# Reading context and x straight from the inputs instead of from copies in DRAM, in a fused mLSTM and FP4 FFN kernel

## The chip, the core and the metric

The kernel runs on one core of one Trainium2 chip. A core has a matrix engine (PE, with its weight loads PEld), a vector engine (DVE), a scalar engine (ACT), a general engine (POOL) and SyncE (SP), which computes nothing and issues transfers. Each engine works off its own instructions in order and waits on semaphores that others raise. ACT can issue transfers too: its sequencer does that, in the place where they stand in ACT's order. Transfers run on 16 DMA engines that all queues share. The metric is the device time of one execution in microseconds (us), lower is better.

## The reference, cut to what matters

For x and a context of shape (8, 1024, 512) the layer computes an mLSTM cross attention with causal decay gates, then a feed forward part whose matrices and activations are rounded to FP4 in blocks of 16:

```
x = x + xattn(layernorm(x), ctx, ctx, igate, fgate, norm_w)
x = x + ffn(layernorm(x), w_gate, w_up, w_down)

xattn: ig, fg = gates of concat(q, k, v);  log_f_cum = cumsum(log_sigmoid(fg))
       D = exp(log_D - max(log_D));  C = (q k^T / 8) * D
       h = C / max(|sum C|, exp(-max)) @ v;  per-head normalisation, times norm_w
ffn:   fp4_linear(h, w_down),  h = silu(fp4_linear(x, w_gate)) * fp4_linear(x, w_up)
fp4_linear(x, w): both quantised in blocks of 16 (scale = max|.|/6, 8 levels), then x @ w^T
```

The attention has 8 heads of width 64; the inner width of the feed forward part is 1408.

## The kernel before, in words

**Tiles.** The 8 x 1024 tokens make 64 tiles of 128 rows. Tile `t` holds 64 tokens (`t.chunk = t // 4`) of batch `2p` in the upper 64 partitions and of batch `2p + 1` in the lower 64 (`t.p = t % 4`). Four tiles after one another cover the same 64 positions of all 8 batches. Such a group of four is also what the gates are computed for at once.

**Turns.** After a prologue (`sp_start`, `act_start`, `dve_start`, ...), which quantises the weights and brings up the first tiles, every engine runs turns `u` from 10 on, each with a fixed order of steps of several tiles: tile `u + 1` is loaded, `u` gets its first layer norm, `u - 1` is transposed, `u - 5` and `u - 6` are in the attention, `u - 7` to `u - 10` are in the feed forward part. So a turn finishes one tile. The order in a turn is written out by hand for each engine (`sp_turn`, `act_turn`, `dve_turn`, ...). Turns with `u % 4 == 0` also do the gate work of a group of four (called gate turns below), turns with `u % 4 == 1` store its rows of maxima and exponentials (`sp_rows_out`).

**What is loaded.** For each tile from the 10th on: `xb` (x for the first layer norm, `sp_x_in`), `cf` (context in blocks of 32 x 32 so that DVE can transpose it into `cT`, `sp_c_in`, four transfers of 32 rows), `cn` (context rows for `vc`, in which the two batch halves are swapped for every other head, `sp_cn_in`), `x1` (x a second time, for the residual, `sp_x1_in`) and broadcasts of the stored gate rows (`mb_in`, `wb_in`). `xb` goes through DRAM once more (`xh_out`, `xz_in`) to come back in the order that DVE's transpose wants.

**The copies.** In turns with `u % 4 == 1`, up to `u = 57`, ACT issues five transfers from DRAM to DRAM ahead of anything else in its turn (`act_stage_x` at L1081, `act_stage_c` at L1074): x and context of the next group of four tiles are written tile by tile into `x_tiles` and `c_tiles`, context with a third half so that `cn` can be read with its halves swapped. The outermost dimension of each copy is the four tiles; it moves 4 x 64 rows of 2 KB. Two groups of such copies are issued in the prologue. `cf` and `cn` are read from `c_tiles` from tile 8 on, `xb` and `x1` from `x_tiles` from tile 12 on.

**Names that come up.** On ACT: L833 the exponentials of `D` (8 instructions), L958 the layer norm of x (`act_xh`), L1007 `hz` (two pieces at the turn's start), L848 to L869 mean and variance of the second layer norm, whose result POOL's L1232 (`rs`) takes. On POOL: L1268 and L1272 (`nb`, which `act_xh` waits for), L1241 `vc` from `cn`, L1257 `xw` from `wb`. On DVE: L1438 and L1443 round the hidden values, L1483 `xs`, L1420 the output, L1746 the transpose of `cf`. On PE: L592 gate and up products, L689 to L729 the attention's products, L748 to L750 the down product.

Of the kernel before, what the change touches and what calls it, by code (L numbers as in the profile page):

```python
# [9 lines left out]
F32 = mybir.dt.float32  # L10
# [65 lines left out]
def mlstm_fp4_ffn(nc, x, ctx_in, ig_w, ig_b, fg_w, fg_b, norm_w, w_gate, w_up, w_down, out):  # L76
# [20 lines left out]
    warp_dram = nc.dram_tensor("warp_dram", [NT // 4, GR * S2], F32, kind="Internal").ap()  # L97

    x_tiles = nc.dram_tensor("x_tiles", [NT, P, E], F32, kind="Internal").ap()
    c_tiles = nc.dram_tensor("c_tiles", [NT, 3 * S2, E], F32, kind="Internal").ap()  # L100

    def tokens(dram, t, b):
        return dram[2 * t.p + b, t.chunk * S2:(t.chunk + 1) * S2, :]

    with ExitStack() as stack:
# [28 lines left out]
        cT = sb("cT", [P, 8, EC, P])  # L134
# [125 lines left out]
        def state_sum(t, b):  # L260
# [16 lines left out]
            "x_in", "c_in", "cn_in", "x_tiles", "c_tiles", "mb_in", "wb_in", "max_out", "warp_out",  # L277
# [22 lines left out]

        def x_staged(t):
            return t.first >= 12

        def c_staged(t):
            return t.first >= 8

        def x_count(t):
            return 64 + 32 * min(t.first - 3, 8) + 16 * max(t.first - 11, 0)

        def x1_count(t):  # L310
            return 32 * min(t.chunk + 1, 3) + 16 * max(t.chunk - 2, 0)

        def cn_count(t):
            return 64 * min(t.first + 1, 8) + 32 * max(t.first - 7, 0)
# [23 lines left out]
        def sp_stored(e, t):  # L338
            e.wait_ge(S_["out"], t.done())
            for b in range(2):  # L340
                e.dma_start(tokens(out, t, b), ob[t.parity][b * S2:(b + 1) * S2, :]).then_inc(s_stored[t.parity], 16)

        def sp_x1_in(e, t):
            if t.at_start(2):
                e.wait_ge(S_["w_qs"], 3 * NG)
            if t.at_start(3):
                e.wait_ge(S_["w_xn"], 3 * NG)
            if t.has(4):
                e.wait_ge(S_["out"], t.done(4))
            if x_staged(t):  # L350
                e.wait_ge(S_["x_tiles"], 32 * (t.chunk - 2))
                e.dma_start(x1[t.slot % 4][:, :], x_tiles[t.first]).then_inc(s_x1_in[t.slot % 4], 16)
                return
            for b in range(2):
                e.dma_start(x1[t.slot % 4][b * S2:(b + 1) * S2, :], tokens(x, t, b)).then_inc(s_x1_in[t.slot % 4], 16)
# [10 lines left out]
        def sp_x_in(e, t):  # L366

            if t.first < 4:
                for b in range(2):
                    e.dma_start(xin(t)[b * S2:(b + 1) * S2, :], tokens(x, t, b)).then_inc(S_["x_in"], 16)  # L370
                return
# [4 lines left out]
            if x_staged(t):  # L376
                e.wait_ge(S_["x_tiles"], 32 * (t.chunk - 2))
                e.dma_start(xb[:, :], x_tiles[t.first]).then_inc(S_["x_in"], 16)
                return
            for b in range(2):  # L380
                e.dma_start(xb[b * S2:(b + 1) * S2, :], tokens(x, t, b)).then_inc(S_["x_in"], 16)
# [15 lines left out]
        def sp_c_in(e, t):  # L397
            if not blocked(t):
                if t.has(1):
                    e.wait_ge(S_["c_T"], t.done(1))  # L400
                for b in range(2):
                    e.dma_start(cf[b * S2:(b + 1) * S2, :], tokens(ctx_in, t, b)).then_inc(S_["c_in"], 16)
                return
            e.wait_ge(S_["cT"], t.done(1))
            e.wait_ge(S_["c_tiles"], 48 * (t.chunk - 1))
            rows = c_tiles[t.first][0:P, :].rearrange("(q s) (k g f) -> g s k q f", s=SQ, g=P // SQ, f=SQ)
            for g in range(P // SQ):
                e.dma_start(cf[g * SQ:(g + 1) * SQ, :].rearrange("s (k q f) -> s k q f", k=EC, f=SQ), rows[g]).then_inc(S_["cz_in"], 16)

        def sp_mb_in(e, t):  # L410
# [4 lines left out]
            e.wait_ge(S_["max_out"], t.dma(4))  # L415
            for k in range(2):
                at = (4 * k + t.p) * NH * S2
                e.dma_start(mb[k * S2:(k + 1) * S2, :, :].rearrange("p h s -> p (h s)"),
                            max_dram[t.chunk:t.chunk + 1, at:at + NH * S2].broadcast_to([S2, NH * S2])).then_inc(S_["mb_in"], 16)
# [12 lines left out]
        def sp_rows_out(e, t):  # L432
            if t.slot % 4 == 3:
# [3 lines left out]
                e.dma_start(warp_dram[t.chunk, :].rearrange("(r s) -> r s", s=S2), mw[:, 1, :]).then_inc(S_["warp_out"], 16)  # L437

        def sp_wb_in(e, t):
# [5 lines left out]
            e.wait_ge(S_["warp_out"], t.dma(4))  # L445
            for par in range(2):
                for b in range(2):
                    at = (((par ^ b) * 4 + t.p) * 2 + par) * HC * S2
                    e.dma_start(wb[par * DH:(par + 1) * DH, b, :, :].rearrange("p c s -> p (c s)"),
                                warp_dram[t.chunk:t.chunk + 1, at:at + HC * S2].broadcast_to([DH, HC * S2])).then_inc(S_["wb_in"], 16)  # L450

        def sp_cn_in(e, t):
# [3 lines left out]
            if c_staged(t):  # L456
                e.wait_ge(S_["c_tiles"], 48 * (t.chunk - 1))
                for par in range(2):
                    e.dma_start(cn[:, :].rearrange("s (c r d) -> s r c d", r=2, d=DH)[:, par],
                                c_tiles[t.first][par * S2:par * S2 + P, :].rearrange("s (c r d) -> s r c d", r=2, d=DH)[:, par]).then_inc(S_["cn_in"], 16)  # L460
                return
            for par in range(2):
                for b in range(2):
                    k = par ^ b
                    e.dma_start(cn[k * S2:(k + 1) * S2, :].rearrange("s (c r d) -> s r c d", r=2, d=DH)[:, par],
                                tokens(ctx_in, t, b).rearrange("s (c r d) -> s r c d", r=2, d=DH)[:, par]).then_inc(S_["cn_in"], 16)
# [25 lines left out]
        def sp_turn(e, u):  # L492
# [11 lines left out]
            if t6.live(NT):  # L504
                sp_cn_in(e, t6)
# [13 lines left out]
            if t6.live(NT):  # L519
                sp_x1_in(e, t6)  # L520
# [74 lines left out]
        def pe_qk(e, t):  # L595
# [1323 lines left out]
```

## Time and profile before

| | us |
|---|---|
| median of 2 runs | 2229.48 (2228.14 to 2230.83) |
| the profiled execution | 2230.32 |
| its span, first to last instruction | 2228.6 |

In that span DVE is busy for 1811.8 us (81%), PE for 1752.1 (79%), POOL for 1220.3 (55%) and ACT for 1154.4 (52%). The span is what the trace shows; the profiled execution's own time is 1.7 us longer. Busy is the time in which an engine executes an instruction, also where that instruction is held up inside by another engine. "Idle before" and the name behind it tell which event ended an engine's idle time.

### The profile page before, as it was taken

What the parts mean: (1) busy time and instruction counts of PE and PEld (TensorE: products, weight loads), DVE (VectorE), ACT (ScalarE), POOL (GpSimd) and SP (SyncE); (2) the same over time, 40 slices, a digit from 0 to 9 for tenths busy, and PEclk for the clock granted to TensorE, in tenths of its full rate; (3) what the DMA queues carried; (4) which work ended last, traced back from release to release, by engine and by line L of the source; (5) the groups of instructions that cost most, each with busy time, mean ns of one, the idle gap of its engine ahead of it and who ended that gap; (6) DMA issues with size and microseconds to landing.
All of it is one profiled execution on the core that took longest, in us unless ns stands there. A gap on an engine that the chain in (4) does not pass through costs nothing. (4 is left out here: it accounts for less than half of the span.)

```text
span 2228.6 us, 46871 instructions
## 1 busy us (share of the span) xinstructions
PE 1752.1 (79%) x16113; PEld 912.3 (41%) x16113; DVE 1811.8 (81%) x3327; ACT 1154.4 (52%) x2602; POOL 1220.3 (55%) x1260
## 2 busy tenths in 40 slices
PE   4444887869879696887869878686987869989998
PEld 3322443434434343443434444343443434444443
DVE  7953986959789695986969689595987959999996
ACT  7643553545555363563645456363554645655542
POOL 7843654636456463654546465463654646666663
PEclk8566988989989898998989989898999989999999
DMA  6395545546455564646545465554645545554333
GB/s 185 90 116 78 127 105 132 122 112 122 120 124 119 128 123 110 136 113 131 120 117 124 112 132 117 126 126 115 132 109 125 122 123 121 117 119 86 88 77 63
DMA packets 647726, 259.86 MB, mean 117 GB/s; under 512 B 581248, under 2 KB 603264, under 8 KB 646944
## 3 DMA queue, kind: packets, MB, share of 16 engines
q1 hardware_dynamic: 646672, 221.21, 48.6%
q10 hardware_dynamic: 816, 35.65, 3.8%
q8 instruction: 128, 2.10, 0.4%
q14 instruction: 110, 0.90, 0.1%
HBM read 159.22 MB, written 67.37 MB: 102 GB/s over the span
## 5 line engine op out<-in xcount | busy, mean ns | idle before, releaser
L592 PE MATMUL bank<-wgTh,xqT 128*128 128x512 f16 (+1 forms) x1536 | 579.7, 377 | 165.0 <-DMA xqT<-xqs 107.0
L592 PE MATMUL bank<-wuTh,xqT 128*128 128x512 f16 (+1 forms) x1536 | 578.0, 376 | 0.0
L1224 POOL TENSOR_TENSOR stage<-stage,hs 128x512 f32<-128x512 f32 (+1 forms) x192 | 213.4, 1111 | 304.4 <-DVE stage L1443 303.1
L592 PEld LDWEIGHTS bank<-wgTh,xqT 128*128 128x128 f16 x1536 | 155.0, 101 | 351.3 <-DMA xqT<-xqs 97.4
L592 PE MATMUL bank<-wgTl,xqT 128*128 128x512 f16 (+1 forms) x768 | 288.9, 376 | 0.0
L592 PE MATMUL bank<-wuTl,xqT 128*128 128x512 f16 (+1 forms) x768 | 288.2, 375 | 0.0
L748 PE MATMUL bank<-wdTh,work 128*128 128x512 f16 x704 | 269.8, 383 | 23.1 <-DMA work<-stage 22.6
L749 PE MATMUL bank<-wdTl,work 128*128 128x512 f16 x704 | 268.6, 382 | 0.0
L750 PE MATMUL bank<-wdTh,work 128*128 128x512 f16 x704 | 268.4, 381 | 0.0
L1279 POOL TENSOR_TENSOR stage<-stage,hinv 128x512 f32<-128x512 f32 (+1 forms) x192 | 210.5, 1109 | 30.7 <-DVE hinv L1542 24.1
L592 PEld LDWEIGHTS bank<-wuTh,xqT 128*128 128x128 f16 x1536 | 155.5, 101 | 154.4 <-issue 19.0
L1483 DVE TENSOR_SCALAR xs<-xam,rs 128x32 f32<-128x32 f32 x64 | 206.9, 3233 | 2.2
L934 ACT ACTIVATE junk<-xb 128x512 bf16<-128x512 f32 x60 | 37.8, 629 | 321.3 <-DMA xb<-x_tiles 313.4
L1241 POOL TENSOR_TENSOR vc<-cn,cols 128x512 f32<-128x512 f32 x64 | 66.8, 1043 | 231.4 <-DMA cn<-c_tiles 202.1
L1462 DVE SCALAR_TENSOR_TENSOR stage<-bank,wfix,stage 128x512 f32<-128x512 f32 (+1 forms) x192 | 134.1, 698 | 68.5 <-ACT stage L886 68.4
L689 PE MATMUL bank<-St,xw 64*64 64x65 f32 x2048 | 54.4, 248 | 170.5 <-DVE mb_D L1454 167.2
L886 ACT ACTIVATE stage<-bank,wfix 128x512 f32<-128x512 f32 (+1 forms) x192 | 124.5, 648 | 115.4 <-PE bank L592 113.4
L1746 DVE STREAM_TRANSPOSE cT<-cf 128x512 f32<-128x512 f32 x55 | 38.4, 698 | 171.4 <-DMA cf<-c_tiles 171.4
L1443 DVE SCALAR_TENSOR_TENSOR stage<-work,stage 128x512 f32<-128x512 bf16 (+1 forms) x192 | 164.0, 881 | 2.3
L1497 DVE TENSOR_TENSOR stage<-stage 128x512 f16<-128x512 f32 (+1 forms) x192 | 134.3, 699 | 37.6 <-ACT stage L876 37.6
L1204 POOL TENSOR_TENSOR sch<-ve,mhalf 128x8 f32<-128x8 f32 x64 | 106.2, 1659 | 98.9 <-DVE ve L1660 98.9
L1218 POOL TENSOR_TENSOR St<-St,wb 128x520 f32<-128x520 f32 x64 | 73.9, 1154 | 143.6 <-PE bank L695 143.6
(215 smaller groups left out, 3978.2 us busy)
## 6 DMA issues: line engine op xcount, KB each, us to landing
wb<-warp_dram SPq DMA_DIRECT2D x256, 64.0 KB, 2.9
mb_D<-max_dram SPq DMA_DIRECT2D x128, 128.0 KB, 3.2
out_dram<-ob SPq DMA_DIRECT2D x128, 128.0 KB, 2.4
cn<-c_tiles SPq DMA_DIRECT2D x112, 128.0 KB, 2.9
xh_dram<-xb SPq DMA_DIRECT2D x55, 256.0 KB, 2.4
xzb<-xh_dram SPq DMA_DIRECT2D x220, 64.0 KB, 2.5
cf<-c_tiles SPq DMA_DIRECT2D x220, 64.0 KB, 2.5
xb<-x_tiles SPq DMA_DIRECT2D x52, 256.0 KB, 2.7
```

What stands on the lines that cost most here:

```text
L592: i = e.matmul(o[:, 0:width], x, w[:, c, n0:n0 + width], start=first and k < 2, stop=last and k >= 4)
L748: e.matmul(acc[:, :], hi, wdT[0][:, c0 + c, :], start=(c0 + c == 0), stop=False)
L749: e.matmul(acc[:, :], hi, wdT[1][:, c0 + c, :], start=False, stop=False)
L750: i = e.matmul(acc[:, :], lo, wdT[0][:, c0 + c, :], start=False, stop=(c0 + c == IC - 1))
L886: e.activation(sl[:, n0:n0 + w], pair(t, n)[0][:, 0:w], ACT.Silu, scale=wfix[:, 0:1]).then_inc(s_silu[n], 1)
L1204: e.tensor_tensor(sch[:, :], ve[:, :], mhalf[:, :], ALU.pow).then_inc(S_["sch"], 1)
L1224: e.tensor_tensor(blocks(hx[:, n0:n0 + w]), blocks(hx[:, n0:n0 + w]), per_block(hs2[:, n0 // BLOCK:(n0 + w) // BLOCK]), ALU.mult).then_inc ...
L1279: e.tensor_tensor(blocks(hx[:, n0:n0 + w]), blocks(hb[:, n0:n0 + w]), per_block(hinv[:, n0 // BLOCK:(n0 + w) // BLOCK]), ALU.mult).then_in ...
L1443: e.scalar_tensor_tensor(hx[:, n0:n0 + w], hz[:, n0:n0 + w], MAGIC, hx[:, n0:n0 + w], ALU.max, ALU.subtract).then_inc(s_h_q[n], 1)
L1462: e.scalar_tensor_tensor(hb[:, n0:n0 + w], pair(t, n)[1][:, 0:w], wfix[:, 1:2], sl[:, n0:n0 + w], ALU.mult, ALU.mult).then_inc(s_h[n], 1)
L1483: e.tensor_scalar(xs[:, :], xam[:, :], rs2[:, :], 6.0 * XS * 1e-12, ALU.mult, ALU.max).then_inc(S_["xs"], 1)
L1497: e.tensor_tensor(hqs[n][:, 1, :], hx[:, n0:n0 + w], hqs[n][:, 0, :], ALU.subtract).then_inc(s_h_lo[n], 1)
```

## The change

The copies in DRAM, their tensors and semaphores are gone. Every load of x and context reads the input itself, with one transfer for each batch half: `xb` and `x1` in 2 transfers of 64 rows where there was 1 of 128, `cf` in 8 of 32 rows with half the columns each where there were 4, `cn` in 4 of 64 rows where there were 2 of 128. `cT` gets a dimension for the batch half, and the products that read it follow. `wb` comes in 2 transfers instead of 4, for which the stored row is written half again behind itself (one more transfer per group). In the turns, `cn` and `x1` are issued by ACT instead of SP: `cn` right behind `act_xh`, `x1` in the middle of the turn. In the prologue SP still issues them.

```diff
-        def tokens(dram, t, b):
-            return dram[2 * t.p + b, t.chunk * S2:(t.chunk + 1) * S2, :]
+    def tokens(dram, t):
+        return dram[2 * t.p:2 * t.p + 2, t.chunk * S2:(t.chunk + 1) * S2, :]
...
-            if x_staged(t):
-                e.wait_ge(S_["x_tiles"], 32 * (t.chunk - 2))
-                e.dma_start(xb[:, :], x_tiles[t.first]).then_inc(S_["x_in"], 16)
-                return
             for b in range(2):
-                e.dma_start(xb[b * S2:(b + 1) * S2, :], tokens(x, t, b)).then_inc(S_["x_in"], 16)
+                e.dma_start(xb[HALF[b], :], tokens(x, t)[b]).then_inc(S_["x_in"], 16)
...
-            e.wait_ge(S_["c_tiles"], 48 * (t.chunk - 1))
-            rows = c_tiles[t.first][0:P, :].rearrange("(q s) (k g f) -> g s k q f", s=SQ, g=P // SQ, f=SQ)
+            rows = tokens(ctx_in, t).rearrange("b (q s) (k g f) -> g b s k q f", s=SQ, g=P // SQ, f=SQ)
             for g in range(P // SQ):
-                e.dma_start(cf[g * SQ:(g + 1) * SQ, :].rearrange("s (k q f) -> s k q f", k=EC, f=SQ), rows[g]).then_inc(S_["cz_in"], 16)
+                for b in range(2):
+                    e.dma_start(cf[g * SQ:(g + 1) * SQ, b * E // 2:(b + 1) * E // 2].rearrange("s (k q f) -> s k q f", k=EC, f=SQ), rows[g, b]).then_inc(S_["cz_in"], 16)
...
+            for par in range(2):
+                row = warp_dram[t.chunk, :].rearrange("(k n r i) -> k n r i", k=3, n=4, r=2)[par:par + 2, t.p, par, :]
+                e.dma_start(wb[par * DH:(par + 1) * DH, :, :, :].rearrange("p b c s -> p (b c s)"),
+                            row.unsqueeze(0).broadcast_to([DH, 2, HC * S2])).then_inc(S_["wb_in"], 16)
+
+        def cn_load(e, t):
+            if t.has(1):
+                e.wait_ge(S_["vc"], t.done(1))
+                e.wait_ge(S_["st_mm"], t.done(1))
+            to = cn[:, :].rearrange("p (c r d) -> p r c d", r=2, d=DH)
+            rows = tokens(ctx_in, t).rearrange("b s (c r d) -> r b s c d", r=2, d=DH)
             for par in range(2):
                 for b in range(2):
...
+                    e.dma_start(to[HALF[par ^ b], par], rows[par, b]).then_inc(S_["cn_in"], 16)
...
         def act_turn(e, u):
             tn = Tile(u + 1)
-            g = (u + 3) // 4
-            if u % 4 == 1 and 4 * g < NT:
-                act_stage_x(e, g)
-                act_stage_c(e, g)
...
             if t0.live(NT):
                 act_xh(e, t0)
+            if t6.live(NT):
+                cn_load(e, t6)
             if t9.live(NT):
                 act_hz(e, t9, 1)
...
             if t9.live(NT):
                 act_hz(e, t9, 2)
                 act_h_hi(e, t9, 1)
+            if t6.live(NT):
+                x1_load(e, t6)
```

The next piece is SP's order in one turn of the middle of the run (`xqT` opens the turn; `cf` and `cn` are context, `x` is the second load of x), before:

```order
L430 DMA_TRANSPOSE xqT<-xqs 128x8x128
L459 DMA cn<-c_tiles 128x4x64 x2
L449 DMA wb<-warp_dram 64x256 x4
L408 DMA cf<-c_tiles 32x16x32 x4
L387 DMA xh_dram<-xb 128x512
L378 DMA xb<-x_tiles 128x512
L395 DMA xzb<-xh_dram 32x16x32 x4
L341 DMA out_dram<-ob 64x512 x2
L352 DMA x<-x_tiles 128x512
L364 DMA_TRANSPOSE work<-stage 128x8x128 x2
```

And the same stretch of the changed program:

```order
L402 DMA_TRANSPOSE xqT<-xqs 128x8x128
L422 DMA wb<-warp_dram 64x2x256 x2
L381 DMA cf<-in_ctx_dram 32x8x32 x8
L360 DMA xh_dram<-xb 128x512
L354 DMA xb<-in_x_dram 64x512 x2
L368 DMA xzb<-xh_dram 32x16x32 x4
L322 DMA out_dram<-ob 64x512 x2
L341 DMA_TRANSPOSE work<-stage 128x8x128 x2
```

`cn` and `x` have left SP's queue, `wb` has two issues less, `cf` four more and `xb` one more: 16 issues in this stretch, which were 17.

The second place is the start of ACT's turn, from the exponentials of `D` to the variance of the second layer norm, with the semaphores that each instruction waits for, before:

```order
L833 ACTIVATE mb_D<-mb_D,cols 128x64 x7
L958 ACTIVATE xb<-xb,nb,rs 128x512 [waits s_ln1,s_ln1_nb]
L1007 ACTIVATE work<-stage 128x512 [waits s_h_q1,s_hx1]
L848 ACTIVATE nm<-sum 128x1 [waits s_x1]
L1007 ACTIVATE work<-stage 128x512 [waits s_h_q0,s_hx0]
```

And in the changed program:

```order
L797 ACTIVATE mb_D<-mb_D,cols 128x64 x7
L922 ACTIVATE xb<-xb,nb,rs 128x512 [waits s_ln1,s_ln1_nb]
L433 DMA cn<-in_ctx_dram 64x4x64 [waits s_st_mm,s_vc]
L433 DMA cn<-in_ctx_dram 64x4x64 x3
L971 ACTIVATE work<-stage 128x512 [waits s_h_q1,s_hx1]
L812 ACTIVATE nm<-sum 128x1 [waits s_x1]
L971 ACTIVATE work<-stage 128x512 [waits s_h_q0,s_hx0]
```

Four transfers now stand between the layer norm of x and the first `hz`.

## Rows read from the trace of the kernel before

**Rows 1.** The page, section 3: each DMA queue's packets, MB, share of 16 engines.
```profile
q1 hardware_dynamic: 646672, 221.21, 48.6%
q10 hardware_dynamic: 816, 35.65, 3.8%
```

**Rows 2.** The waits of the whole span: us in total, times, longest us.
```profile
PE bank L689 <- DVE mb_D L1454: 167.2, 12, 15.0
```

**Rows 3.** Windows, `u % 4 == 1` turns 13 to 57: busy us by engine, PEclk, DMA.
```profile
319.62:366.99 47.37, 26.13 (x229) 13.49 (x228) 24.49 (x49) 15.81 (x40) 17.94 (x19) 0.78 0.47 124
...
sum 560.69, PE 321.58 PEld 165.84 DVE 294.83 ACT 190.60 POOL 215.31; mean PE 26.80 PEld 13.82 DVE 24.57 ACT 15.88 POOL 17.94
```

**Rows 4.** The same view of turns 61, 10 and 60.
```profile
1918.65:1946.15 27.50, 25.94 (x241) 13.17 (x240) 27.19 (x49) 16.51 (x40) 17.69 (x19) 1.00 0.63 125
...
230.29:257.92 27.63, 24.57 (x226) 12.33 (x227) 26.88 (x47) 14.50 (x34) 17.52 (x18) 0.94 0.56 118
1886.41:1918.65 32.24, 29.53 (x298) 15.81 (x296) 28.17 (x55) 20.66 (x46) 17.76 (x19) 0.95 0.47 106
```

**Rows 5.** Timeline of SP's queue, turn 37 (with copies) and turn 38.
```profile
1122.74 22.70 SPq L449 DMA_DIRECT2D wb<-warp_dram  x4
...
1169.07 2.58 SPq L449 DMA_DIRECT2D wb<-warp_dram  x4
1171.74 3.71 SPq L408 DMA_DIRECT2D cf<-c_tiles  x4
```

**Rows 6.** Timeline of ACT and its queue at the start of turn 33.
```profile
986.38 0.35 ACT L833 ACTIVATE mb_D<-mb_D,cols 128x64 f32<-128x64 f32 x1
986.40 0.62 ACTq L1081 DMA_DIRECT2D x_tiles<-in_x_dram  x1
...
988.35 1.57 ACTq L1074 DMA_DIRECT2D c_tiles<-in_ctx_dram  x2
990.03 0.81 ACT L958 ACTIVATE xb<-xb,nb,rs 128x512 f32<-128x512 f32 x1 [1.64 <-issue]
```

**Rows 7.** Timeline of ACT, turns 34, 60 and 61, in that order.
```profile
1037.53 0.63 ACT L1007 ACTIVATE work<-stage 128x512 bf16<-128x512 f32 x1 [0.71 <-POOL stage L1279]
...
1892.44 0.20 ACT L848 ACTIVATE nm<-sum 128x1 f32<-128x1 f32 x1 [0.94 <-DVE x L1432]
...
1922.26 0.63 ACT L1007 ACTIVATE work<-stage 128x512 bf16<-128x512 f32 x1 [0.20 <-POOL stage L1279]
...
1923.72 0.63 ACT L1007 ACTIVATE work<-stage 128x512 bf16<-128x512 f32 x1 [0.29 <-POOL stage L1279]
```

**Rows 8.** Timeline of POOL, turn 34 and turn 61.
```profile
1034.75 0.26 POOL L1272 TENSOR_TENSOR nb<-nm,rs 128x1 f32<-128x1 f32 x1
...
1039.65 0.85 POOL L1232 TENSOR_TENSOR rs<-ss,mhalf 128x1 f32<-128x1 f32 x1 [1.54 <-ACT ss L869]
...
1045.01 1.26 POOL L1257 TENSOR_TENSOR xw<-xT,wb 128x512 f32<-128x512 f32 x1
...
1920.95 0.26 POOL L1272 TENSOR_TENSOR nb<-nm,rs 128x1 f32<-128x1 f32 x1
```

**Rows 9.** Timeline of DVE, turn 34, then its long idle times in the prologue.
```profile
1041.32 4.99 DVE L1483 TENSOR_SCALAR xs<-xam,rs 128x32 f32<-128x32 f32 x1
...
135.53 0.69 DVE L1731 TENSOR_TENSOR work<-stage,work 128x512 f16<-128x512 f32 x1 [9.78 <-ACT work L1066]
...
169.19 0.45 DVE L1630 SCALAR_TENSOR_TENSOR nr<-uc,cols 128x8 f32<-128x8 f32 x1 [12.22 <-ACT uc L1028]
...
180.56 0.28 DVE L1572 TENSOR_TENSOR_SCAN F<-f_neg,f_log 64x64 f32<-64x64 f32 x1 [9.15 <-ACT f_log L997]
```

**Rows 10.** ACT's queue in the prologue, its first copy.
```profile
111.88 1.22 ACTq L1074 DMA_DIRECT2D c_tiles<-in_ctx_dram  x1
```

**Rows 11.** The page, section 6: KB each, median us from issue to landing.
```profile
xb<-x_tiles SPq DMA_DIRECT2D x52, 256.0 KB, 2.7
...
xb<-in_x_dram SPq DMA_DIRECT2D x16, 128.0 KB, 2.7
```

More of the change, by code:

```diff
@@ L340, in sp_stored, with x1_load @@
             for b in range(2):
-                e.dma_start(tokens(out, t, b), ob[t.parity][b * S2:(b + 1) * S2, :]).then_inc(s_stored[t.parity], 16)
-        def sp_x1_in(e, t):
+                e.dma_start(tokens(out, t)[b], ob[t.parity][HALF[b], :]).then_inc(s_stored[t.parity], 16)
+        def x1_load(e, t):
             if t.at_start(2):
@@ L349, in sp_x1_in @@
                 e.wait_ge(S_["out"], t.done(4))
-            if x_staged(t):
-                e.wait_ge(S_["x_tiles"], 32 * (t.chunk - 2))
-                e.dma_start(x1[t.slot % 4][:, :], x_tiles[t.first]).then_inc(s_x1_in[t.slot % 4], 16)
-                return
             for b in range(2):
-                e.dma_start(x1[t.slot % 4][b * S2:(b + 1) * S2, :], tokens(x, t, b)).then_inc(s_x1_in[t.slot % 4], 16)
+                e.dma_start(x1[t.slot % 4][HALF[b], :], tokens(x, t)[b]).then_inc(s_x1_in[t.slot % 4], 16)
         def sp_hqT(e, t, n):
@@ L415, in sp_mb_in @@
             e.wait_ge(S_["max_out"], t.dma(4))
+            row = max_dram[t.chunk, :].rearrange("(k n r) -> k n r", k=2, n=4)[:, t.p, :]
             for k in range(2):
-                at = (4 * k + t.p) * NH * S2
-                e.dma_start(mb[k * S2:(k + 1) * S2, :, :].rearrange("p h s -> p (h s)"),
-                            max_dram[t.chunk:t.chunk + 1, at:at + NH * S2].broadcast_to([S2, NH * S2])).then_inc(S_["mb_in"], 16)
+                e.dma_start(mb[HALF[k], :, :].rearrange("p h s -> p (h s)"), row[k].unsqueeze(0).broadcast_to([S2, NH * S2])).then_inc(S_["mb_in"], 16)
         def sp_xqT(e, t):
@@ L436, in sp_rows_out @@
                 e.wait_ge(S_["warp"], t.quads())
[L437 removed]
+                again = warp_dram[t.chunk, :].rearrange("(r s) -> r s", s=S2)
+                e.dma_start(again[0:GR, :], mw[:, 1, :]).then_inc(S_["warp_out"], 16)
+                e.dma_start(again[GR:GR + QR, :], mw[0:QR, 1, :]).then_inc(S_["warp_out"], 16)
         def sp_wb_in(e, t):
@@ L444, in sp_wb_in @@
                 e.wait_ge(S_["xw"], t.done(1))
-            e.wait_ge(S_["warp_out"], t.dma(4))
+            e.wait_ge(S_["warp_out"], 2 * t.dma(4))
             for par in range(2):
[L447 to L452, printed above, removed]
+                row = warp_dram[t.chunk, :].rearrange("(k n r i) -> k n r i", k=3, n=4, r=2)[par:par + 2, t.p, par, :]
+                e.dma_start(wb[par * DH:(par + 1) * DH, :, :, :].rearrange("p b c s -> p (b c s)"),
+                            row.unsqueeze(0).broadcast_to([DH, 2, HC * S2])).then_inc(S_["wb_in"], 16)
+        def cn_load(e, t):
             if t.has(1):
@@ L651, in pe_gate_mm @@
                     for two in range(2):
-                        for part, src in enumerate((xT, cT)):
+                        pair_of = slice(t.slot - 3 + 2 * two, t.slot - 1 + 2 * two)
+                        for part, src in enumerate((xT[:, pair_of, c, :].rearrange("p t (b s) -> p t b s", b=2), cT[:, pair_of, :, c, :])):
                             at = 32 * (2 * two + part)
-                            first = t.slot - 3 + 2 * two
-                            i = e.matmul(gates(t)[0][at:at + 32, :].rearrange("p (t s) -> p t s", t=2), gT[:, part * EC + c, :],
-                                         src[:, first:first + 2, c, :], start=(c == 0), stop=(c == EC - 1))
+                            i = e.matmul(gates(t)[0][at:at + 32, :].rearrange("p (t b s) -> p t b s", t=2, b=2), gT[:, part * EC + c, :],
+                                         src, start=(c == 0), stop=(c == EC - 1))
                 i.then_inc(S_["gate_mm"], 1)
@@ L904, in act_cT @@
                 e.wait_ge(S_["qk"], t.done(8))
-            e.copy(cT[:, t.slot, :, :].rearrange("p c s -> p (c s)"), R1[:, :]).then_inc(S_["cT"], 1)
+            e.copy(cT[:, t.slot, :, :, :].rearrange("p b c s -> p c b s"), R1[:, :].rearrange("p (c b s) -> p c b s", c=EC, b=2)).then_inc(S_["cT"], 1)
         def act_x_hi(e, t):
@@ L928, in act_ln1_sum @@
             if t.has(4):
-                e.wait_ge(S_["x_in"], x_count(t))
+                e.wait_ge(S_["x_in"], 64 + 32 * (t.first - 3))
             else:
@@ L1741, in dve_cT @@
         def dve_cT(e, t):
-            e.wait_ge(S_["cz_in"], 64 * (t.first - 8))
+            e.wait_ge(S_["cz_in"], 128 * (t.first - 8))
             if t.at_start(9):
```

82 lines of the change are left out of this document (21 added, 61 removed).

## Prediction

> **What bounds the kernel now.** I read the DMA queues first, then the waits, then windows cut at the turns, and last the timelines of a few turns.
>
> The queue table shows two very different queues [rows 1]. SP's q1 moves 221 MB in 646,672 packets, about 340 bytes each. ACT's q10 holds only the copies: 35.65 MB in 816 packets, 43.7 KB each, and its time is 3.8% of 16 engines' span, 1,355 us of engine time. 68 copies (13 groups of 5, and 3 more for context group 2) share that: 19.9 us each. At 26 GB/s per engine such a packet takes 1.7 us, some hundred times as long as one of SP's.
>
> The waits then show something that comes 12 times and costs 14 us each [rows 2], and 12 is the number of turns in which ACT issues copies. Cut at SP's `xqT`, these 12 turns take 560.69 us, 46.7 each, with PEclk down to 0.8 and DVE busy for only 24.6 [rows 3]. Turn 61 is my control: a turn with `u % 4 == 1` and all its other steps, `sp_rows_out` among them, but with no copies left to issue. It takes 27.50 us [rows 4]. In a turn with copies SP's queue stands still in the four issues of `wb` for 22.70 us, where the next turn needs 2.58 [rows 5]. So SP cannot issue while the large packets occupy the DMA engines, everything behind `wb` (context, x, the transposes) comes late, and all engines idle.
>
> A turn without copies is bounded by another thing: DVE is busy for 27.19 of 27.50 us [rows 4], but 4.99 of those are `xs`, a 128 x 32 operation [rows 9]. It ends at 1046.31, just as POOL finishes an unbroken train of operations with `xw` at 1046.27 [rows 8]. So DVE is held by POOL there. That train starts with `rs` at 1039.65, 1.54 after POOL fell idle, and waits for ACT's variance [rows 8]. The loop that sets the turn is thus: DVE, POOL's `nb`, the start of ACT's turn, ACT's variance, POOL's train, DVE. Time added at ACT's start counts, beyond small covers.
>
> **What is removed.** Twelve turns fall from 46.7 to 27.5: 560.69 - 12 x 27.50 = **230.7 us**. In the prologue DVE idles 9.78, 12.22 and 9.15 us [rows 9] right behind its first eight copies, 31.2 in all; some would be lost to other waits, so I take **28**, with bounds 10 and 45 (further waits follow until 215 us).
>
> **What SP gains and pays.** Per turn SP loses `cn` and `x1` (3 issues) and 2 of `wb`, and gets 4 for `cf` and 1 for `xb`: the count stays. At 2.58/4 = 0.65 each for `wb` and 3.71/4 = 0.93 for `cf` [rows 5], context starts one `cn` pair and two `wb` earlier and has four issues more, so `xh_out` stands where it stood, within 1 us. The second half of `xb` costs one issue more, 0.65, against an ACT that will be later anyway: nothing. The halved loads have been seen: in turn 10 x still came in halves and the turn took 27.63 [rows 4], and halves land after 2.7 us as whole tiles do [rows 11]. The Trainium skill, page "DMA: Bandwidth & Descriptors", section "Rules for kernel authors", speaks against them: two transfers to disjoint partition halves serialize, one transfer for 128 partitions is better. The row shows 0.13 us per turn at most; if the halves did follow each other by a full 2.7 us, ACT's next steps would slip by up to 1 us beyond their cover in 54 turns, some 50 us.
> The extra issue of `rows_out`, the new layout of `cT` and the split column order in the gate products move no bytes and add no instruction on DVE or PE: nothing. They stand beside 20 us of PE products per turn.
>
> **What ACT pays.** `x1`'s two issues come where ACT idles in every turn (after `hz` 2, before `xz`), and they wait for the output of tile `u - 10`, which DVE has done right after `xs`: nothing. `cn` is the cost. Its waits (`vc` and the state product of the tile before) are met some 6 us earlier. When can it issue? In turn 33 the first copy is issued at 986.40, with the first of the 8 exponentials of `D` (986.38), while the other seven still run [rows 6]. So ACT's sequencer issues as soon as the waits of all instructions ahead are met, not when they are done. Ahead of `cn` the last one that waits is `act_xh`, for POOL's `nb`. That is done at 1034.75 + 0.26 = 1035.01 in turn 34 [rows 8]. Four issues at 0.62 to 0.70 (the five copies take 3.52 from 986.40 to 989.92 [rows 6]) make 2.64, until 1037.65; the next instruction starts 0.1 behind the last issue (990.03 behind 989.92 [rows 6]).
> - Ordinary turns (28 of the turns 10 to 63): first `hz` 1037.75 to 1038.38, second `hz` 1038.4 instead of 1037.53 [rows 7]; the 0.71 that it had waited for POOL covers part. Variance, `rs` and POOL's train move by **0.9**.
> - Turns with `u % 4 == 1` (13): `nb` is done at 1921.21 [rows 8], `cn` until 1923.85, the first `hz` at 1923.95 instead of 1922.26, the second, 1922.26 to 1923.72 less its own 0.29 wait behind it [rows 7], at 1925.12: **1.4**.
> - Gate turns (13): there the mean waits 0.94 for DVE [rows 7], which eats the 0.9: **0**.
> - Turns 64 to 69 have no layer norm of x; the issue hides under the exponentials: **0**.
>
> Sum: 28 x 0.9 + 13 x 1.4 = **43 us**. From below the bound is 0 (the covers take it all), from above four issues at 1.22 us each, the price of the first copy of all [rows 10].
>
> **The sum**: 2230.3 (the profiled execution) - 230.7 - 28 + 43 = **2015 us**. The median of the runs is 0.8 below that execution, which changes nothing.
>
> **Rivals.**
> - *Absorbed (chance 0.2).* DVE's 4.99 us in `xs` is a wait for a gap in POOL's work. POOL's idle time before `rs` grows from 1.54 to 2.4 us, and DVE's order against POOL's shifts by half a microsecond. If DVE gets in earlier, or `nb`'s wait does not hold the issue back (then `cn` would start with the exponentials and end 1.5 us sooner), ACT's delay costs nothing: 2230.3 - 230.7 - 28 = 1972, and down to 1935 if DVE wins some 0.7 per turn in 54 turns. Against it: 4.99 is the same in nearly every ordinary turn. Page "SBUF — State Buffer" of the Trainium skill, section "Who interferes with whom", has it that whichever of the two starts first holds the shared ports for its whole instruction; it does not say who wins between two back-to-back operations, so it changes no chance.
> - *Dear issues (0.18).* SP and ACT issue at the same time now. In turn 33, two of the copies took 1.57 [rows 6], 0.79 each, while SP issued too. At 0.79 plus gaps `cn` takes 3.4, 0.7 more per turn, in 54 turns 38: 2053. At 1.22 plus gaps it takes 5.1, 2.4 more: 2145. Page "Perfetto Trace Analysis", section "DMA Instruction — HWDGE (DVE, Sync)", tells that one descriptor generator is shared and locked for each issue, which is how this would happen; the traces have no turn with both queues at work for long. Serial halves (2065, above) fall in this case too.
> - *SP becomes the bound (0.03), slower.* Same cause at full price in SP's queue: 25 issues per turn at 1.22 [rows 10] are 30.5 us, and the wait for `xh_out` to land, 2.7 by the load of the same size [rows 11], makes 33.2 per turn, 5.7 more than now, in 60 turns 342: 2230.3 - 258.7 + 342 = 2314. It decides from a mean issue of about 1.2 us on: then SP's turn is over 27.5 + 4.3, and the gain of 259 is used up. `wb` at 0.65 and `cf` at 0.93 [rows 5] speak against it.
> - *The stalls are not the copies' (0.02), slower.* Then they stay, in whatever else happens in these turns, and ACT's cost is paid: 2273. Turn 61 speaks against it.
> - *Part of it (0.07)*: between 2085 and 2230, a shorter stall left in turns with `u % 4 == 1`, or several small costs.
>
> **Numbers.** The forecast has 0.5, with its own range of 1990 to 2050. With most of "absorbed" and the cheaper half of "dear issues" the range is **1955 to 2085**, which leaves out the deepest gain, issues near 1.22 us, and both slow cases, about 0.2. About 2% is what a measurement can tell from no change; 2185 and below is faster, at **0.92**, within 2% **0.04**, slower **0.04**.
>
> **What would show it.** Right: no turn longer than a gate turn; ordinary turns at 28.4, turns with `u % 4 == 1` at 28.9, gate turns at 31 to 32; `wb`'s issue never above 2 us; the first `cn` issue within 0.1 us of `nb`'s end and the first `hz` idle for "issue" for about 1.7; `xs` still near 5. Wrong: a `cn` issue starting with the exponentials or behind `act_xh`; `cn` taking over 3 us; `xb` landing late, so that ACT's L934 waits grow; PE waiting for `xqT`.

## The result, and the profile after

| | before | changed |
|---|---|---|
| median, us | 2229.48 | 2009.59 (2005.50 to 2013.67) |
| the profiled span, us | 2228.6 | 2003.7 |
| ratio of the times | | 0.9017, 95% interval 0.8982 to 0.9051 |

The forecast was 2015, the range 1955 to 2085. Where the 224.9 us of the span came from is seen by cutting it at SP's `xqT`, as for [rows 3, 4]. Sums of all turns of a kind, in us, with the mean of one:

| stretch | before | changed | difference |
|---|---|---|---|
| until turn 10 | 230.3 | 197.7 | -32.6 |
| gate turns (`u % 4 == 0`), 13 | 411.3 (31.6) | 417.7 (32.1) | +6.4 |
| `u % 4 == 1`, 13 | 588.2 (45.2) | 376.7 (29.0) | -211.5 |
| `u % 4 == 2`, 14 | 385.1 (27.5) | 396.6 (28.3) | +11.5 |
| `u % 4 == 3`, 14 | 386.3 (27.6) | 392.5 (28.0) | +6.2 |
| turn 64 to the end | 227.4 | 222.5 | -4.9 |

The queues of the changed kernel, the page's section 3 (packets, MB, share of 16 engines), answer to [rows 1]. q10 carries small packets now, ACT's share of the loads:

```profile
q1 hardware_dynamic: 577488, 189.88, 44.9%
q10 hardware_dynamic: 74880, 31.48, 6.3%
```

The windows of the turns 13 to 57 with `u % 4 == 1`, the first and the sum of 12, answer to [rows 3] (length, busy time of each engine, PEclk, DMA share, GB/s):

```profile
286.35:315.17 28.82, 25.87 (x241) 13.06 (x240) 27.89 (x49) 16.34 (x40) 17.71 (x19) 1.00 0.56 119
...
sum 347.89, PE 311.72 PEld 156.52 DVE 335.11 ACT 194.12 POOL 212.55; mean PE 25.98 PEld 13.04 DVE 27.93 ACT 16.18 POOL 17.71
```

DVE was busy for 24.6 of 46.7 us there and is now busy for 27.9 of 29.0: the stall is gone. What remains above the 27.5 of the control turn starts with ACT. Its timeline at the start of turn 41 (start, us, instruction, idle time before it), and below it POOL's and SP's:

```profile
1113.31 2.02 ACT L797 ACTIVATE mb_D<-mb_D,cols 128x64 f32<-128x64 f32 x8
1115.47 0.81 ACT L922 ACTIVATE xb<-xb,nb,rs 128x512 f32<-128x512 f32 x1
1115.54 2.59 ACTq L433 DMA_DIRECT2D cn<-in_ctx_dram  x4
1118.22 0.63 ACT L971 ACTIVATE work<-stage 128x512 bf16<-128x512 f32 x1 [1.94 <-issue]
```

```profile
1115.18 0.26 POOL L1221 TENSOR_TENSOR nb<-nm,rs 128x1 f32<-128x1 f32 x1
...
1121.41 0.97 POOL L1181 TENSOR_TENSOR rs<-ss,mhalf 128x1 f32<-128x1 f32 x1 [2.88 <-ACT ss L833]
```

```profile
1112.88 1.23 SPq L402 DMA_TRANSPOSE xqT<-xqs  x1
1114.23 1.26 SPq L422 DMA_DIRECT2D wb<-warp_dram  x2
```

The first `cn` issue starts 0.10 us after `nb` has ended at 1115.44, while `act_xh` is at work. It holds the first `hz` for 1.94 us, and POOL waits 2.88 us for the variance where it waited 1.54 [rows 8]. `wb` issues in 1.26 instead of 22.70 [rows 5]. DVE's timeline has `xs` in two forms, in turn 41 and in turn 42:

```profile
1120.68 1.29 DVE L1392 SCALAR_TENSOR_TENSOR stage<-work,stage 128x512 f32<-128x512 bf16 x2
...
1122.60 5.49 DVE L1432 TENSOR_SCALAR xs<-xam,rs 128x32 f32<-128x32 f32 x1
...
1150.22 4.58 DVE L1392 SCALAR_TENSOR_TENSOR stage<-work,stage 128x512 f32<-128x512 bf16 x2
...
1155.43 0.54 DVE L1432 TENSOR_SCALAR xs<-xam,rs 128x32 f32<-128x32 f32 x1
```

In the first form `xs` is held, 4.95 us longer than in the second; in the second the pair at `L1392` is held, 3.29 us longer than in the first, so this form loses less. In ordinary turns (`u % 4` is 2 or 3) the second form makes 27.8 to 27.9 us and the first 28.4 to 29.2. Of the 28 ordinary turns 16 have the second form, of the 13 gate turns 4; all turns with `u % 4 == 1` have the first.

### The profile page after: what moved, and what is told of

The parts are those of the page before. It is cut to its first block and busy times, and to the rows that moved or that the text cites. A ratio compares the mean times of both kernels' runs of the same rounds, so it can differ in the third digit from the quotient of the medians.

```text
span 2003.7 us, 46968 instructions
## 1 busy us (share of the span) xinstructions
PE 1721.4 (86%) x16113; PEld 893.4 (45%) x16113; DVE 1865.8 (93%) x3327; ACT 1154.1 (58%) x2602; POOL 1219.8 (61%) x1260
## 5 line engine op out<-in xcount | busy, mean ns | idle before, releaser
L712 PE MATMUL bank<-wdTh,work 128*128 128x512 f16 x704 | 268.5, 381 | 12.3 <-DMA work<-stage 12.2
L1432 DVE TENSOR_SCALAR xs<-xam,rs 128x32 f32<-128x32 f32 x64 | 220.9, 3451 | 2.2
L1392 DVE SCALAR_TENSOR_TENSOR stage<-work,stage 128x512 f32<-128x512 bf16 (+1 forms) x192 | 190.6, 1019 | 2.3
L971 ACT ACTIVATE work<-stage 128x512 bf16<-128x512 f32 (+1 forms) x192 | 112.2, 585 | 124.6 <-issue 71.2
L856 ACT ACTIVATE xz<-xn 128x512 bf16<-128x512 f32 x64 | 40.3, 629 | 216.5 <-DVE xn L1450 216.5
L1167 POOL TENSOR_TENSOR St<-St,wb 128x520 f32<-128x520 f32 x64 | 71.2, 1113 | 132.7 <-PE bank L659 132.7
L840 ACT CAST stage<-stage 128x512 f16<-128x512 f32 (+1 forms) x192 | 110.7, 577 | 60.7 <-POOL stage L1173 57.4
L1181 POOL TENSOR_TENSOR rs<-ss,mhalf 128x1 f32<-128x1 f32 x64 | 51.0, 797 | 155.3 <-ACT ss L833 155.3
L1411 DVE SCALAR_TENSOR_TENSOR stage<-bank,wfix,stage 128x512 f32<-128x512 f32 (+1 forms) x192 | 134.2, 699 | 11.5 <-ACT stage L850 11.3
L1387 DVE SCALAR_TENSOR_TENSOR stage<-work,stage 128x512 f32<-128x512 bf16 (+1 forms) x192 | 120.2, 646 | 24.5 <-ACT work L971 24.3
```

The source lines that it names most:

```text
L712: e.matmul(acc[:, :], hi, wdT[0][:, c0 + c, :], start=(c0 + c == 0), stop=False)
L971: e.activation(hz[:, n0:n0 + w], hx[:, n0:n0 + w], ACT.Abs, scale=FP4_ONE).then_inc(s_hz[n], 1)
L1387: e.scalar_tensor_tensor(hx[:, n0:n0 + w], hz[:, n0:n0 + w], MAGIC, hx[:, n0:n0 + w], ALU.max, ALU.add).then_inc(s_h_t[n], 1)
L1392: e.scalar_tensor_tensor(hx[:, n0:n0 + w], hz[:, n0:n0 + w], MAGIC, hx[:, n0:n0 + w], ALU.max, ALU.subtract).then_inc(s_h_q[n], 1)
L1411: e.scalar_tensor_tensor(hb[:, n0:n0 + w], pair(t, n)[1][:, 0:w], wfix[:, 1:2], sl[:, n0:n0 + w], ALU.mult, ALU.mult).then_inc(s_h[n], 1)
L1432: e.tensor_scalar(xs[:, :], xam[:, :], rs2[:, :], 6.0 * XS * 1e-12, ALU.mult, ALU.max).then_inc(S_["xs"], 1)
```

## The experiments

Two questions were open. What in the copies made the stall: their bytes, their number, or their form? And what do ACT's issues really cost, in their place and elsewhere? All ratios are to the kernel before, run beside each kernel.

### The copies: form, not bytes

**The copies kept, but described row by row.** In the kernel before, each copy writes 4 tiles of 64 rows, with the tiles outermost. Here the rows are outermost, bytes and number as they were:

```diff
-e.dma_start(x_tiles[4 * g:4 * g + 4, k * S2:(k + 1) * S2, :], src[k])
+e.dma_start(x_tiles[...].rearrange("t s e -> s t e"), src[k].rearrange("t s e -> s t e"))
...
```

`[...]` stands for the index of the line above, and the copies of the context are changed in the same way. (The expectation speaks of ten copies a group; there are five.)

> The kernel before, its ten DRAM-to-DRAM copies of each group kept with all their bytes, but each described row by row (64 rows of the sequence outermost, 4 tiles of 2 KB in each) instead of tile by tile (4 outermost, each 128 KB in one piece). Theory A, the stall of 19.2 us in the 12 copy turns comes from copies that fall to few of the 16 engines in large packets, in front of which SyncE's issues wait: the stall goes or shrinks to a few us, 2010 to 2060 us. Rival B, the stall is the bytes of the copies (35.65 MB for the whole run) in any form: 2215 to 2240. Rival C, it is the issues' count and time on ScalarE: 2215 or more.

2015.25 us, ratio 0.9045 (0.9029 to 0.9061). One `rearrange` on the copies, and the kernel before is as fast as the changed one within the intervals. Theory A held. The queue's rows of this kernel:

```profile
q1 hardware_dynamic: 646672, 221.21, 52.6%
q10 hardware_dynamic: 18496, 35.66, 5.6%
```

**Four groups of 16 rows, and sixteen groups of 4 rows.** The first shortens the contiguous piece and leaves 4 elements outermost; the second puts 16 outermost.

```diff
+e.dma_start(x_tiles[...].rearrange("t (a s) e -> a t (s e)", a=4), src[k].rearrange("t (a s) e -> a t (s e)", a=4))
```

> The kernel before with its DRAM-to-DRAM copies described in 4 groups of 16 rows outermost and 32 KB in one piece, in place of 4 tiles with 128 KB in one piece. If the length of the pieces makes the stall in proportion (2 KB: none; 128 KB: 19.2 us a turn): 2040 to 2200 us. If a copy with 4 outermost elements stalls whatever their length: 2200 to 2240.

> The same with 16 groups of 4 rows outermost, 8 KB in one piece. If 16 outermost elements are enough: the stall is gone as with 64 rows, 2010 to 2025 us. If 2 KB pieces were what helped: between, 2040 to 2150.

With `a=4`: 2225.77 us, 0.9976 (0.9966 to 0.9987). With `a=16`: 2015.51, 0.9041 (0.9023 to 0.9060). Quartering the contiguous piece took 0.2% off; with 16 outermost elements, in pieces of 8 KB, the stall was gone. The page's row of q10 for `a=4`, then for `a=16`:

```profile
q10 hardware_dynamic: 1360, 35.65, 3.8%
```

```profile
q10 hardware_dynamic: 5440, 35.66, 5.2%
```

Divide by the 68 copies: 20 packets a copy with `a=4` and 80 with `a=16`; 12 in the kernel before [rows 1] and 272 row by row. The pieces of 32, 8 and 2 KB account for 16, 64 and 256 of these. What is over is 4, 16 and 16. Each engine that takes part seems to add one packet, so that with 4 outermost elements only 4 of the 16 engines carry the copy. (The 12 of the kernel before would then be 4 and 8 packets of 64 KB.) The Trainium skill, page "DMA: Bandwidth & Descriptors", section "Why a DMA increments its semaphore by 16 and not by 1", says so outright: the number of engines is the largest up to 16 that divides the slowest dimension of both sides. The counts and the times agree with it. So does the share of the 16 engines' time that q10 fills while copies run: 24.9% from 990 to 1012 us in the kernel before and 24.6% in 22 us of turn 33 with `a=4`, which is 4 of 16, but 88.9% in 6 us of turn 33 with `a=16` and 88.0% row by row.

The sizes fit. Five copies are 2.5 MB (5 x 512 KB). On four engines at the 26 GB/s each that [rows 1] give (35.65 MB in 1,355 us of engine time), that is some 25 us; on sixteen, 6. The DMA view of the kernel before from 984 to 1010 us, in turn 33, shows DMA engines that are mostly idle while SP stands still in `wb` from 989 to 1012 (the upper row is the mean busy share of 16 engines in tenths, 40 slices):

```profile
DMA  0000199605492009000900190072007200720090
...
q10 hardware_dynamic: 52, 2.36, 21.6%
q1 hardware_dynamic: 2008, 0.57, 10.3%
```

The same stretch with the copies row by row:

```profile
DMA  0001999899999999997888778900394165587969
...
q1 hardware_dynamic: 7640, 2.45, 43.7%
q10 hardware_dynamic: 1360, 2.62, 31.1%
```

More bytes in the same time, four times as many by SP, and SP's `wb` is issued in 2.54 us. Not all of the hold is gone: `cf`, right behind it, takes 7.84 us there, and in the 12 turns `xh_out` comes 12.2 to 14.2 us after `xqT`, against 8.0 to 9.7 in turns without copies.

One rival is left by the times: that pieces of 32 KB and more stall, and pieces of 8 KB and less don't. No run has long pieces on 16 engines.

**The copies put back into the changed kernel**, their data unread, all five of a turn or only the two of x (without the last line shown):

```diff
 def act_turn(e, u):
+    if u % 4 == 1 and 4 * g < NT:
+        act_stage_x(e, g)
+        act_stage_c(e, g)
...
```

> The changed kernel with the five copies of each of the 12 turns put back (two of x, three of the context), issued by ScalarE where the kernel before issues them; nothing reads what they write. Theory A, the copies alone make the stall: 12 times 17 to 20 us more, 2210 to 2245 us. Rival B, the stall came from the loads that wait for copies to land or from the loads' form in the kernel before: 2005 to 2040 us.

> The changed kernel with only the two copies of x put back in each of the 12 turns; nothing reads them. Two fifths of the bytes. Theory A with a stall in proportion to bytes: 12 times 7.7, 2095 us. Theory A', the issuing queue takes some copies before it holds: little, 2005 to 2050 us. Rival B, copies don't stall: 2003 to 2015 us.

Five: 2240.62 us, 1.0061 (1.0045 to 1.0078). Two: 2071.88, 0.9302 (0.9288 to 0.9316). So the copies stall a kernel that doesn't read them, and its other loads are the new ones: rival B is out. Theory A's range for five held. For two, the measured time lies between A's figure and the range of A', and both missed. SP's timelines in turn 33, with five copies:

```profile
972.27 1.65 SPq L424 DMA_DIRECT2D wb<-warp_dram  x2
973.97 26.56 SPq L383 DMA_DIRECT2D cf<-in_ctx_dram  x8
```

and with two:

```profile
908.02 1.47 SPq L424 DMA_DIRECT2D wb<-warp_dram  x2
909.55 12.22 SPq L383 DMA_DIRECT2D cf<-in_ctx_dram  x8
```

SP is held in `cf`, which takes 6.65 us in turn 33 without copies, for 20 us more with 640 KB on each of four engines and for 6 more with 256 KB. The 12 turns take 563.5 and 394.9 us instead of 347.9, 18.0 and 3.9 more each. The first few us of a hold fall into SP's idle time ahead of the next `xqT`, which shrinks from 4.3 us in turn 33 to 0.7 and 0.6; most of the rest is paid. With the two copies the 12 turns hold 47 of the 62 us by which the whole run is longer; turns with `u % 4 == 3` are 10 us longer in all, and gate turns 8, which is hardly more than two traces of the changed kernel differ by in them (7).

### ACT's issues: the place, not the count

**The changed kernel once more**, beside the next three.

> The changed kernel once more, as the measure for the three that run beside it. Both theories: 2005 to 2010 us, 0.90 of the kernel before.

2010.15 us, 0.9019 (0.8981 to 0.9057).

**`cn` issued by SP**, ahead of `wb`:

```diff
 def sp_turn(e, u):
     if t6.live(NT):
+        cn_load(e, t6)
         sp_wb_in(e, t6)
...
 def act_turn(e, u):
-    if t6.live(NT):
-        cn_load(e, t6)
```

> The changed kernel with the four context-row transfers (cn) of a turn given back to SyncE, right ahead of its wb transfers; x's second load stays with ScalarE. Theory A: ScalarE's issues (2.56 us a turn, of which 24 us in all were seen in the turns) stand on the way from the norm's scale to the first hz; without them the ordinary turns go back from 28.2 to 27.5 us and the time falls by 20 to 30 us, to about 1983. Rival B, the issues lie in idle time of ScalarE: no change, 2003 to 2012. Rival C, SyncE cannot carry four issues more (its queue then holds wb back): slower than the changed kernel, 2030 or more.

2000.23 us, 0.8986 (0.8967 to 0.9006). That is 10 below the run beside it, but the intervals overlap, so against the changed kernel it is undecided; theory A's 1983 was missed. The waits tell why (us in total, times, longest). In the changed kernel:

```profile
ACT work L971 <- issue: 71.2, 35, 3.0
...
PE bank L712 <- DMA work<-stage: 12.2, 3, 8.9
```

With `cn` on SP:

```profile
ACT junk L899 <- DMA xb<-in_x_dram: 293.3, 56, 7.2
...
PE bank L713 <- DMA work<-stage: 52.3, 30, 8.9
```

The wait for issue is gone from ACT, which now waits 293.3 us for `xb` instead of 129.8. PE waits 40 us longer for SP's transposes of `h_q`, which stand 2.6 us further back in SP's row. One wait took the other's place.

**`cn` issued by ACT, but later in its turn**, behind the sum of squares, for the next tile:

```diff
-    if t6.live(NT):
+    if u == FIRST:
         cn_load(e, t6)
...
     if t6.live(NT):
         act_sq(e, t6)
+    if t5.live(NT):
+        cn_load(e, t5)
     if t7.live(NT):
         act_x_hi(e, t7)
```

> The changed kernel with the same four transfers still issued by ScalarE, but a stretch later: behind the sum of squares for the context's step and ahead of x_hi of the tile before, where ScalarE was seen idle for about 2 us, and so nearly one turn earlier than the tile needs them. Theory A (it is the place of the issues that costs, not the issues): 1980 to 1990 us, ordinary turns 27.5 to 27.7. Rival B (issues cost nothing where they are): 2003 to 2012. Rival D (2.56 us of ScalarE cost the same wherever they stand, because ScalarE's whole order is tight): 2003 to 2015 too, but with the wait before the first hz gone and another of about the same size in its place.

2020.73 us, 0.9070 (0.9054 to 0.9087): slower than in its old place, and than every range given. Rival D's picture fits: ACT's wait for issue before `hz` fell from 71.2 us to 2.0, and another came. ACT's timeline in turn 35:

```profile
958.67 0.63 ACT L1001 ACTIVATE sq<-uc 128x512 f32<-128x512 f32 x1
958.76 3.25 ACTq L433 DMA_DIRECT2D cn<-in_ctx_dram  x4
962.11 0.62 ACT L878 CAST xqs<-xn 128x512 f16<-128x512 f32 x1 [2.80 <-POOL xn L1213]
```

Four issues took 3.25 us, 0.81 each, and `xqs`, on which SP's next `xqT` waits, could start only behind them. The idle time there was 0.9 to 2.1 us, and the new load didn't fit. The label names POOL, since its semaphore came last; the instruction starts 0.1 behind the issue. In 30 other turns the view does name the issue:

```profile
ACT xqs L878 <- issue: 79.1, 30, 3.7
```

But turn 35 took only 27.56 us. Ordinary turns take 27.7 on average here, which is theory A's figure; turns with `u % 4 == 1` take 30.0 and gate turns 32.8, against 27.5 and 31.1 in the two-buffer kernel below. So the loss lies in those two kinds of turn, and how the late `xqs` makes it there was not followed. Nor was what makes four issues last from 2.55 to 4.13 us in this place.

**Eight issues instead of four**, each transfer cut in two of 32 rows:

```diff
-e.dma_start(to[HALF[par ^ b], par], rows[par, b])
+for q in range(2):
+    low = S2 * (par ^ b) + 32 * q
+    e.dma_start(to[low:low + 32, par], rows[par, b][32 * q:32 * q + 32])
...
```

> The changed kernel with each of the four context-row transfers cut in two of 32 rows: eight issues by ScalarE a turn, the same bytes. Theory A, the issues are on the path: another 2.6 us a turn on ScalarE, now none of it covered: 2.0 to 2.6 us times 54 to 60 turns, 2115 to 2160 us. Rival B, idle time takes them: 2003 to 2030. Rival C, the number of transfers costs through the queues and not through the engine: slower too, but with ScalarE's issue not longer than 2.6 us before the first hz.

2221.93 us, 0.9990 (0.9975 to 1.0004). That eats the whole gain, and is dearer than theory A's upper end. ACT in turn 38:

```profile
1132.54 5.25 ACTq L435 DMA_DIRECT2D cn<-in_ctx_dram  x7
1137.89 0.63 ACT L973 ACTIVATE work<-stage 128x512 bf16<-128x512 f32 x1 [4.76 <-issue]
```

ACT's wait grew by 2.8 us against turn 41 of the changed kernel, and ordinary turns by 3.1 to 4.0, from 28.3 and 28.0 to 31.5 and 32.0. The mean granted clock of TensorE fell with it, from 0.953 to 0.900 of full speed, and PE's busy time rose from 1722.2 to 1787.9 us. That is 1 us a turn, and may be the part above the issue time; no run takes it apart.

**Two buffers for `cn`.** ACT's longest idle time is ahead of the first sum over the next x, where it waits for `xb` to land. `cn` can't be issued there as long as the tile before still uses its buffer, so it gets a second one, and a semaphore for each:

```diff
-cn = sb("cn", [P, E])
+cn = [sb(f"cn{i}", [P, E]) for i in range(2)]
...
 def cn_load(e, t):
-    if t.has(1):
-        e.wait_ge(S_["vc"], t.done(1))
-        e.wait_ge(S_["st_mm"], t.done(1))
+    if t.has(2):
+        e.wait_ge(S_["vc"], t.done(2))
+        e.wait_ge(S_["st_mm"], t.done(2))
...
-    if t6.live(NT):
+    if u == FIRST:
         cn_load(e, t6)
...
+    if t5.live(NT):
+        cn_load(e, t5)
     if tn.live(NT):
         act_ln1_sum(e, tn)
```

> The changed kernel with two buffers for the context rows (cn), so that ScalarE can issue a tile's four transfers a turn earlier, ahead of the first sum over the next x, where it was seen idle for 3 to 6.5 us waiting for xb to land. If the four issues cost only where they meet work of ScalarE: no wait for issue before the first hz, ordinary turns 27.5 to 27.7 us, u%4==1 and gate turns 1 us shorter, 1965 to 1985 us. If four issues cost wherever ScalarE makes them, as they did when they were moved behind the sum of squares (2021 us): 2005 to 2025. If only the transfers and their bytes count: 2000 to 2010.

**The same, issued by SP** behind the third transpose of `h_q`, in SP's idle time:

> The same two buffers, the four transfers issued by SyncE behind the third h_q transpose of a turn, where it was seen idle for 4.3 us ahead of the next xqT. If the cost of cn_on_sp was that SyncE's row of issues made the h_q transposes 2.6 us late: that goes too, 1960 to 1980 us. If four more issues on SyncE delay the next xqT in the gate turns, where its row is longest: gate turns over 33 us, 2000 or more.

1964.79 us, 0.8810 (0.8795 to 0.8825), and 1962.00, 0.8802 (0.8787 to 0.8818). Both beat the changed kernel, whose interval starts at 0.8981; 0.8810 by 0.9019 is 0.977. ACT in turn 36:

```profile
948.79 0.56 ACTq L434 DMA_DIRECT2D cn<-in_ctx_dram  x1
...
949.38 2.05 ACTq L434 DMA_DIRECT2D cn<-in_ctx_dram  x3
953.60 0.63 ACT L899 ACTIVATE junk<-xb 128x512 bf16<-128x512 f32 x1 [2.95 <-DMA xb<-in_x_dram]
```

The issues end at 951.43, and `xb` lands 2 us later. `hz` waits 0.19 for POOL, POOL's `rs` waits 1.54 for the variance, as in [rows 8], and the windows of the same 12 turns, the second and the sum:

```profile
402.71:430.21 27.50, 25.94 (x241) 12.99 (x240) 27.19 (x49) 16.51 (x40) 17.70 (x19) 1.00 0.58 125
...
sum 329.99, PE 305.28 PEld 154.02 DVE 326.25 ACT 197.86 POOL 212.38; mean PE 25.44 PEld 12.84 DVE 27.19 ACT 16.49 POOL 17.70
```

They repeat the control turn [rows 4], the busy times of DVE, ACT and POOL included. SP in turn 35 of the other kernel, where the four issues end 0.7 ahead of the next `xqT`:

```profile
933.48 2.54 SPq L434 DMA_DIRECT2D cn<-in_ctx_dram  x4
936.74 1.25 SPq L403 DMA_TRANSPOSE xqT<-xqs  x1
```

**Eight issues in that idle time.** The dearest number in the cheapest place: the kernel with two buffers and ACT's issues, with the cut of the eight-issue kernel.

> The kernel with two buffers for the context rows and ScalarE's issues in its idle stretch (1965 us), each of the four transfers cut in two of 32 rows, as in the eight-issue kernel that took 2222 us. There the eight stood on the way to the first hz. If an issue costs only where it meets work of ScalarE: eight take 5.2 us, and the idle stretch is about 4.9 us (949.35 to 953.60 and the 0.6 ahead of it), so next to nothing, 1963 to 1985 us. If the number of transfers costs by itself, through the queues and engines that carry them: near 212 us more, 2150 or more.

1971.76 us, 0.8842 (0.8827 to 0.8857): 7 more for the same four extra issues that cost 212 in the other place. ACT in turn 34:

```profile
897.54 4.52 ACTq L436 DMA_DIRECT2D cn<-in_ctx_dram  x7
902.16 0.63 ACT L901 ACTIVATE junk<-xb 128x512 bf16<-128x512 f32 x1 [4.40 <-DMA xb<-in_x_dram]
```

The idle time is used up, to 0.1 us. Of the 7 us, 2.5 lie in turn 10, where the first tile's load is still issued ahead of `hz` (32.02 against 29.49 us). So the number of transfers is nearly free in itself; what costs is the issuing engine's work that stands behind them.

## Why the prediction was right, point by point

- **What is removed, 230.7.** Exact. In the kernel with two buffers the 12 turns take 329.99, and 560.69 - 329.99 is 230.70. The step "down to the control turn" held to 0.1 us. The reason given for the stall was half right. It was the copies, and SP could not issue behind them. But I put it on packet length ("some hundred times as long as one of SP's"; [rows 1] give 62 times), and 32 KB pieces stall as 128 KB pieces do. The step that failed is the reading of the queue's 3.8%: that is a mean over 16 engines, and I did not ask how many of them had the work. Five copies of 19.9 us of engine time are 99.5 us, 25 on each of four engines and 6 on each of sixteen, and SP stood still for 22.70. Hence I didn't see that one line mends the kernel before, and that the rewrite as a whole gains nothing measurable beyond that. Copies on all engines still cost their turns 3.7 us (31.2 against 27.5), 44 in all, about what ACT's issues cost the changed kernel; with those out of the way (1965) the copies' removal does show.
- **The prologue, 28.** Measured 32.6. With the copies kept but 16 or 64 outermost, turns 8 and 9 already fall from 113.4 to 86.2 and 86.3, so most of it is form as well; with `a=4` they take 112.3.
- **SP, nothing.** Right for the changed kernel: `cf`'s eight issues take 5.8 us by the median of the turns, and `xh_out` comes 8.1 to 9.4 us after `xqT`, where it came after 8.0 to 9.7 in the turns without copies. The 3.71 us that I took for four issues of `cf` was a dear turn; their median before is 2.66. The number of SP's issues in the stretch shown stays at 22, as the prediction has it; the 16 and 17 given with the change are miscounted. It is no free ground, though: four issues more in front of `wb` cost PE 40 us of waits.
- **The halved loads, nothing.** Right: an `xb` transfer of 64 rows lands in 2.6 us by the median of the changed kernel, one of 128 rows took 2.7 [rows 11]. ACT's waits for `xb` fell from 313.4 to 129.8 us in total, since those of the stalls are gone. That two halves follow each other, as the page of the Trainium skill in the prediction has it, shows in no row here, and the rival that rested on it (2065) has nothing for it.
- **ACT's issues, 43.** The total was right, the parts were not, so that it came out is partly luck. Against the two-buffer kernel, the turns 10 to 63 of the changed one take 1583.5 against 1534.1 us: 49.4. Over the span it is 40, since the changed kernel is 2 us faster in the prologue and 7 in the last turns; by the medians it is 45. By kind, predicted and measured: ordinary turns 25 and 17.0; `u % 4 == 1` 18.2 and 19.2; gate turns 0 and 13.2. In a second trace of the same kernel (`after_again`) the first two come out the same within 0.2 us and the gate turns at 6.3; 9 of the 13 have the second form of DVE's timeline there, instead of 4. The zero for the gate turns failed. I let the mean's 0.94 us wait for DVE absorb the issue, but DVE comes behind ACT in the loop that I had described, so its lateness is no cover; that is an argument, no run took this wait apart. Against the kernel before this hides behind a gain of 6.8 us in the same turns that I hadn't seen either. In the ordinary turns I missed that DVE can be held in `L1392` instead of in `xs`, and then loses only 0.3 to 0.4 to the control.
- **Absorbed (0.2).** Part of it came. The issue did wait for `nb`, but in 16 of 28 ordinary turns DVE's order against POOL's did shift, and the turn lost 0.3 to 0.4 us instead of 0.9. Its price, 1972 for no cost of ACT, is close to the 1965 that the two-buffer kernel measured.
- **Dear issues (0.18).** `cn`'s four issues took 2.59 us in turn 41 with both queues at work, 0.65 each, and 2.56 by the median of the turns 11 to 63 (3.63 at most), so not here. Behind the sum of squares they did take 3.25.
- **SP as the bound, stalls not the copies'.** Both out: `wb` never took over 1.6 us from turn 10 on, and no turn with `u % 4 == 1` is longer than 30.0 us.

## What to carry to other kernels

Before removing DRAM-to-DRAM copies, look at their outermost dimension: with 4 elements there, five copies of 512 KB held up the other queue's issues for 20 us while the DMA engines were mostly idle, and with 16 or more they cost 3.7 us a turn. A queue's share of all engines' time doesn't show this over the whole run (3.8%); in a window in which the copies run, it does (24.9%, four of sixteen). The price of a DMA issue here is the work that stands behind it on the issuing engine: four more issues of 0.65 us a turn cost 212 us in one place and 7 in idle time. So find the longest idle time of each issuing engine, and where a buffer is not free by then, try a second one.

## What the runs showed that was not expected

- One `rearrange` on the copies (2015 us) and the whole rewrite (2010) give the same time within the intervals.
- A hold of SP of 6 us costs its turn 3.9, a hold of 20 us costs 18.0: the cover is used up once.
- In the two-buffer kernel with ACT's issues, the 12 turns of the windows take 27.49 to 27.51 us. What sets 27.5, with DVE busy for 27.19 of it and 4.99 of that in `xs`, beside POOL's train, was not tried.
